# A transformer layer's last chunk: projection, layer norm and MLP in two halves of the queries, with the stores on SyncE's queue

## The reference

```python
h = _layernorm(x, ln1_g, ln1_b)
x = x + _mha(h, h, sa_wq, ...)            # 16 heads of 16, self attention
h = _layernorm(x, ln2_g, ln2_b)
x = x + _mha(h, context, ca_wq, ...)      # cross attention, ends in o @ wo.T + bo
h = _layernorm(x, ln3_g, ln3_b)
h = gelu(h @ mlp_w1.T + mlp_b1) @ mlp_w2.T + mlp_b2   # exact gelu, hidden width 1024
return x + h
```

## Time and profile before

| what | value |
|---|---|
| median of 3 runs | 1604.9 us (1602.36 to 1605.7) |
| time of the profiled execution | 1600.0 us |
| span of the profiled execution | 1598.3 us |
| mean granted TensorE clock over the span | 0.963 of full |
| TensorE busy | 1470.2 us (92%) |
| ScalarE busy | 1068.1 us (67%) |
| VectorE busy | 536.6 us (34%) |

### The profile page before, as it was taken

How to read it: one execution, slowest core, us unless ns; L and a number is a source line. 1 busy time by engine, 2 the same in 40 slices (tenths; PEclk the granted TensorE clock), 3 DMA queues, 4 the chain that set the end, 5 groups by cost and what they waited for, 6 DMA issues and landing times.

```text
span 1598.3 us, 21199 instructions
## 1 busy us (share of the span) xinstructions
PE 1470.2 (92%) x8062; PEld 636.2 (40%) x8062; DVE 536.6 (34%) x1286; ACT 1068.1 (67%) x1285; POOL 44.0 (3%) x62
## 2 busy tenths in 40 slices
PE   8889999998874999999999999699999999999967
PEld 5567777776331222322322322232223432432334
DVE  2445555556541022231330431233232133143140
ACT  2323333332433999999999999589788787797831
POOL 2100000000110000000000000000000000000000
PEclk9999999999896999999999999799899999999988
DMA  7300000000496000010010254501000000000000
GB/s 237 145 7 8 6 7 7 7 3 0 97 249 112 11 21 11 11 39 21 11 37 20 31 84 85 112 21 47 12 21 11 25 11 11 21 15 1 7 7 14
DMA packets 37672, 64.07 MB, mean 40 GB/s; under 512 B 6164, under 2 KB 21844, under 8 KB 37428
## 3 DMA queue, kind: packets, MB, share of 16 engines
q1 hardware_dynamic: 32024, 40.87, 12.3%
q0 software_dynamic: 5552, 21.89, 3.8%
HBM read 40.85 MB, written 22.02 MB: 39 GB/s over the span
## 4 chain that ended last, share of the span: by engine, by line
PE 71%; ACT 17%; DVE 4%; DMA 4%; issue 3%; SPq 0%; DVEq 0%; ACTq 0%; POOL 0%; POOLq 0%
PE PS L954 22%; PE PS L937 15%; ACT PX L677 14%; PE PS L756 6%; PE PS L765 6%; PE PS L1011 5%; PE PS L1023 4%; PE PS L994 2%; PE PS L802 2%; DMA k_parts<-KPARTS 2%; PE PS L728 1%; PE PS L774 1%; PE PS L777 1%; PE PS L973 1%; PE PS L732 1%
## 5 line engine op out<-in xcount | busy, mean ns | idle before, releaser
L677 ACT ACTIVATE PX<-PS 128x1024 f32<-128x1024 f32 (+1 forms) x928 | 883.6, 1040 | 163.5 <-PE PS L937 114.3
L954 PE MATMUL PS<-PX,V 128*32 128x512 f32 (+1 forms) x3712 | 499.4, 610 | 5.0 <-ACT PX L677 3.0
L937 PE MATMUL PS<-QST,stack 50*128 50x512 f32 (+1 forms) x1856 | 385.3, 472 | 44.0 <-DMA stack<-k_parts 22.7
L937 PEld LDWEIGHTS PS<-QST,stack 50*128 50x128 f32 (+1 forms) x1856 | 155.8, 185 | 445.2 <-ACT PX L677 342.6
L954 PEld LDWEIGHTS PS<-PX,V 128*32 128x32 f32 (+1 forms) x3712 | 73.7, 108 | 152.1 <-issue 126.3
L1373 DVE COPY OT<-PS 128x512 f32<-128x512 f32 x32 | 22.1, 692 | 313.0 <-PE PS L954 311.7
L604 ACT ACTIVATE PR<-PS,small 128x1601 f32<-128x1601 f32 x16 | 25.6, 1597 | 106.8 <-DVE small L1210 106.8
L756 PE MATMUL PS<-tokF,XT 128*128 128x512 f32 (+1 forms) x256 | 95.0, 525 | 0.6 <-DVE small L1142 0.6
L765 PE MATMUL PS<-tokT,PT 128*128 128x256 f32 (+1 forms) x416 | 93.3, 381 | 0.6 <-DVE CZ L1259 0.6
L765 PEld LDWEIGHTS PS<-tokT,PT 128*128 128x128 f32 (+1 forms) x416 | 77.9, 190 | 10.7 <-issue 0.8
L1023 PE MATMUL PS<-W,HIDT 128*128 128x256 f32 x256 | 65.2, 404 | 10.6 <-ACT HIDT L663 9.8
(11 more groups left out here) (134 smaller groups left out, 1148.6 us busy)
## 6 DMA issues: line engine op xcount, KB each, us to landing
QST<-q_parts SPq DMA_DIRECT2D x192, 64.0 KB
q_parts<-PARTS POOLq DMA_DIRECT2D x16, 512.0 KB, 5.4
stack<-k_parts SPq DMA_DIRECT2D x24, 256.0 KB, 9.7
stack<-k_parts SPq DMA_DIRECT2D x24, 200.1 KB, 7.1
k_parts<-KPARTS POOLq DMA_DIRECT2D x8, 512.0 KB, 12.2
v_cross<-V POOLq DMA_DIRECT2D x1, 3328.0 KB, 10.0
V<-v_cross SPq DMA_DIRECT2D x2, 1664.0 KB, 13.8
k_parts<-PARTS POOLq DMA_DIRECT2D x6, 512.0 KB, 3.4
```

What stands on the lines that cost most here:

```text
L677: act.activation(PX[0:kr, (2 * t + half) % 4, :, :], PS[0:kr, slot:slot + 2, :], ACT.Exp, scale=SCALE).then_inc(at["exp"], 1)
L937: ins = pe.matmul(PS[0:kr, 2 * (n % LOOK) + jj, :], KST[a][lo:lo + NROW, pair, kt * P:kt * P + kr].bitcast(F32R), QST[lo:lo + NROW, pair, ...
L954: ins = pe.matmul(PS[32 * j:32 * j + 32, 6, :], V[0:kr, kt, 2 * (g // 2 * GH + j) + g % 2, :], PX[0:kr, (2 * t + j // 2) % 4, j % 2, :], s ...
```

## The change

Only the last chunk's tail is rewritten.

- The divide: VectorE takes the reciprocal straight from PSUM and multiplies `ONF`, one half of 256 queries after the other (`END = 256`, `END_TILES = 2`).
- The projection of group 1, bias, residual, statistics, inverse square root and standardisation run per half of two tiles. The square root's twelve small steps are so executed twice.
- The transposes run per half, into banks 4 and 5; the scaling to `HC` moves from VectorE to ScalarE (Identity with scale and bias), 256 columns an instruction.
- W1 is multiplied per half, 16 units of 256 columns in place of 8 of 512, through banks 0, 1, 6 and 7; the second half's transposes stand after six units of the first (`END_EARLY = 6`), and its scaling on ScalarE after six Gelus. There are 16 Gelus of 256 columns.
- The output product writes banks 2 to 5; a tile of the first half waits only for the Gelus of the first half.
- `mlp_b2` is added to the residual `X` beforehand, so one addition per tile is left after the product.
- SyncE issues the last four stores, after all its loads; GpSimd's loop ends a chunk earlier.

The core of the diff:

```diff
+        for i in range(TILES - TPC, TILES):
+            sp.wait_ge(A[1]["out_ready"], i + 1)
+            sp.dma_start(out[i * P:(i + 1) * P, :], XH[:, i % TPC, :]).then_inc(S["end_stored"], 16)
+        sp.wait_ge(S["end_stored"], 16 * TPC)
...
-        with gp.Fori(0, CHUNKS) as c:
+        with gp.Fori(0, CHUNKS - 1) as c:
...
+                def end_scaled(half):
+
+                    for i in range(2):
+                        act.wait_ge(at["hT"], 2 * (q + half) + i + 1)
+                        act.activation(HC[:, i, half * END:(half + 1) * END],
+                                       PS[:, END_TURN + i, half * END:(half + 1) * END], ACT.Identity,
+                                       scale=col("L1_xattn_ln3_g", i), bias=col("L1_xattn_ln3_b", i)) \
+                            .then_inc(at["hc"], 1)
+
+                end_scaled(0)
+                act.wait_ge(at["mlp"], q * TPC)
+                for n in range(2 * units):
+                    half, i = n // units, n % units
+                    if n == END_EARLY:
+                        end_scaled(1)
+                    act.wait_ge(at["unit"], units * q + n + 1)
+                    act.activation(HIDT[:, i, half * END:(half + 1) * END],
+                                   PS[:, END_HIDDEN[n % len(END_HIDDEN)], 0:END], ACT.Gelu,
+                                   bias=col("L1_xattn_mlp_b1", i)).then_inc(at["unit_taken"], 1)
...
+            def end_turn(half):
+
+                pe.wait_ge(at["hat"], q + 1 + half)
+                for i in range(2):
+                    for tt in range(half * END_TILES, (half + 1) * END_TILES):
+                        ins = pe.transpose(PS[:, END_TURN + i, tt * P:(tt + 1) * P],
+                                           XH[:, tt, i * P:(i + 1) * P], ident[:])
+                    ins.then_inc(at["hT"], 1)
+
+            def end_hidden(half, i):
+
+                n = half * units + i
+                if i == 0:
+                    pe.wait_ge(at["hc"], 2 * (q + 1 + half))
+                if n >= len(END_HIDDEN):
+                    pe.wait_ge(at["unit_taken"], units * q + n - len(END_HIDDEN) + 1)
+                for c in range(2):
+                    ins = pe.matmul(PS[:, END_HIDDEN[n % len(END_HIDDEN)], 0:END], W1[:, c, i * P:(i + 1) * P],
+                                    HC[:, c, half * END:(half + 1) * END], start=(c == 0), stop=(c == 1))
+                ins.then_inc(at["unit"], 1)
+
+            pe.wait_ge(at["wop"], 16)
+            pe.wait_ge(at["normed"], CHUNKS * GP - 1)
+            for i in range(TPC):
+                end_projection(0, i)
+            for half in range(2):
+                pe.wait_ge(at["normed"], CHUNKS * GP + half)
+                for i in range(half * END_TILES, (half + 1) * END_TILES):
+                    end_projection(1, i).then_inc(at["y"], 1)
+            end_turn(0)
+            for i in range(units):
+                if i == END_EARLY:
+                    end_turn(1)
+                end_hidden(0, i)
+            for i in range(units):
+                end_hidden(1, i)
+            for tt in range(TPC):
+                pe.wait_ge(at["unit_taken"], units * (q + 1 + tt // END_TILES))
+                for k in range(units):
+                    ins = pe.matmul(PS[:, END_OUT[tt], 0:D], HIDT[:, k, tt * P:(tt + 1) * P], W2[:, k, :],
+                                    start=(k == 0), stop=(k == units - 1))
+                ins.then_inc(at["mlp"], 1)
...
+                for half in range(2):
+                    span = slice(half * END, (half + 1) * END)
+                    ch(ve.reciprocal(REC[:, span], PS[:, 7, span]))
+                    ve.tensor_tensor(ONF[:, 1, span], ONF[:, 1, span], REC[:, span], ALU.mult) \
+                        .then_inc(at["normed"], 1)
+                for half in range(2):
+                    tiles = range(half * END_TILES, (half + 1) * END_TILES)
+                    ve.wait_ge(at["y"], q * TPC + (half + 1) * END_TILES)
...
+                    rsqrt(END_TILES, ch, i=half * END_TILES)
+                    for i in tiles:
+                        ins = ve.tensor_scalar(XH[:, i, :], X[:, q * TPC + i, :], sm(AG + 2 * i), sm(NY + i),
+                                               ALU.subtract, ALU.mult)
+                    ins.then_inc(at["hat"], 1)
...
+                    ins = ve.tensor_tensor(X[:, q * TPC + i, :], X[:, q * TPC + i, :], row("L1_xattn_mlp_b2"), ALU.add)
...
+                    ve.wait_ge(at["mlp"], q * TPC + i + 1)
+                    ve.tensor_tensor(XH[:, i, :], PS[:, END_OUT[i], 0:D], X[:, q * TPC + i, :], ALU.add) \
+                        .then_inc(at["out_ready"], 1)
```

More of the change, by code:

```diff
@@ L74 @@
 LOOK = 3
+END = CHUNK // 2
+END_TILES = TPC // 2
+END_HIDDEN = (0, 1, 6, 7)
+END_TURN = 4
+END_OUT = (2, 3, 4, 5)
+END_EARLY = 6
 class Map:
@@ L235, in build @@
         l0_gates l0_rtanh l0_ubiased l0_utanh l0_rps l0_candps l0_candz l0_cand l0_x1
-        ln1_hat ln1_T ln1_taken qkv_unit v_unit_taken out_stored""".split()
+        ln1_hat ln1_T ln1_taken qkv_unit v_unit_taken out_stored end_stored""".split()
     S = {n: sem(n) for n in names}
@@ L556, in _ @@
                     .then_inc(S["out_stored"], 16)
-        gp.wait_ge(S["out_stored"], 16 * TILES)
+        gp.wait_ge(S["out_stored"], 16 * (TILES - TPC))
     @block.scalar
@@ L685, in _ @@
             if a == 1:
[L687 to L694, removed]
+                q = CHUNKS - 1
+                units = HID // P
+                def end_scaled(half):
[15 more added lines that the diff above has]
+                                   bias=col("L1_xattn_mlp_b1", i)).then_inc(at["unit_taken"], 1)
     @block.tensor
@@ L973, in sums, with piece @@
                 pe.matmul(PS[:, 7, :], spread[:], SUMS[:], start=True, stop=True).then_inc(at["sums"], 1)
-            def piece(kind, i, q, part, tail=False, at=at):
-                whole = part is None
-                first, last = whole or part == 0, whole or part == PARTS_OF[kind] - 1
+            def piece(kind, i, q, part, at=at):
+                first, last = part == 0, part == PARTS_OF[kind] - 1
                 def share(n):
-                    if whole:
-                        return range(n)
                     w = n // PARTS_OF[kind]
                     return range(part * w, (part + 1) * w)
-                bank = i % 4 if tail else 7
                 if kind == "y":
@@ L993, in piece @@
                     for g in share(GP):
-                        ins = pe.matmul(PS[:, bank, 0:D], ONF[:, g, i * P:(i + 1) * P], WOP[:, g, :],
+                        ins = pe.matmul(PS[:, 7, 0:D], ONF[:, g, i * P:(i + 1) * P], WOP[:, g, :],
                                         start=(g == 0), stop=(g == GP - 1))
@@ L1000, in piece @@
                     for tt in range(TPC):
-                        ins = pe.transpose(PS[:, bank, tt * P:(tt + 1) * P],
+                        ins = pe.transpose(PS[:, 7, tt * P:(tt + 1) * P],
                                            XH[:, tt, i * P:(i + 1) * P], ident[:])
@@ L1007, in piece @@
                         pe.wait_ge(at["hc"], 2 * q + 2)
-                        if tail and i >= 4:
-                            pe.wait_ge(at["unit_taken"], HID // P * q + i - 3)
                     for c in share(2):
-                        ins = pe.matmul(PS[:, bank, :], (CAWQ if kind == "u" else W1)[:, c, i * P:(i + 1) * P],
+                        ins = pe.matmul(PS[:, 7, :], (CAWQ if kind == "u" else W1)[:, c, i * P:(i + 1) * P],
                                         HC[:, c, :], start=(c == 0), stop=(c == 1))
@@ L1017, in piece @@
                 if kind == "o":
-                    if tail:
-                        pe.wait_ge(at["unit_taken"], HID // P * CHUNKS)
-                    elif first:
+                    if first:
                         pe.wait_ge(at["gelu"], q + 1)
                     for k in share(HID // P):
-                        ins = pe.matmul(PS[:, bank, 0:D], HIDT[:, k, i * P:(i + 1) * P], W2[:, k, :],
+                        ins = pe.matmul(PS[:, 7, 0:D], HIDT[:, k, i * P:(i + 1) * P], W2[:, k, :],
                                         start=(k == 0), stop=(k == HID // P - 1))
@@ L1069, in _ @@
             sums(CHUNKS, 0)
[L1071 to L1083, removed]
+            q = CHUNKS - 1
+            units = HID // P
+            def end_projection(g, i):
+                return pe.matmul(PS[:, i, 0:D], ONF[:, g, i * P:(i + 1) * P], WOP[:, g, :],
+                                 start=(g == 0), stop=(g == GP - 1))
+            def end_turn(half):
[5 more added lines that the diff above has]
+                    ins.then_inc(at["hT"], 1)
@@ L1415, in standardise, with piece @@
                 ve.wait_ge(at["hat"], q + 1)
-            def piece(kind, i, q, tail=False, a=a, at=at):
+            def piece(kind, i, q, a=a, at=at):
                 if kind in "yo":
@@ L1430, in piece @@
                     ve.wait_ge(at["hT"], 2 * q + i + 1)
```

(33 more changed lines are left out.)

## The result

| | before | after |
|---|---|---|
| median | 1604.84 us (1602.32 to 1607.6, 6 runs) | 1592.55 us (1589.79 to 1594.41, 6 runs) |
| profiled execution, span | 1598.3 us | 1589.8 us |
| instructions | 21199 | 21258 |

The two spans differ by only 8.5 us. The spread sums, up to which both kernels run the same code, begin at 1538.25 in one profiled execution and at 1543.33 in the other. So I measure the tail from the start of the spread sums, and compare whole executions by their medians only.

A forecast was written before the change was run, and what follows sets the result against it. The bound was the last 60 us, a chain stepping from engine to engine with nothing beside it. 6.8 - 0.6 + 0.45 + 0.5 = 7.2 us off 1604.9 gave 1597.7 us, range 1593.8 to 1601.5.

The forecast's parts named there:

- After it: Behind the output product: one addition in place of two, 0.45 us won; last store by SyncE, 0.5 us won.
- Division and projection: From the spread sums to VectorE's layer norm: it starts at about 1543.9 in place of 1546.64, 2.7 us won.
- Layer norm of the first half: On VectorE, for two tiles in place of four: 5.7 us in place of 8.56, 2.85 us won.
- Transposes and scaling: Between the layer norm and W1: 1.8 us in place of 2.94, 1.15 us won.
- W1 and output product: TensorE's stretch from the start of W1: 31.9 us against 31.3 before, 0.6 us lost.
- Cover of the second half: Inside W1: second `hat` is ready 1.4 to 3.7 us before TensorE asks for it, so no wait.
- Table load: On ScalarE: Gelu's load of 1.28 us runs behind the first two scalings, 1551.4 to 1552.7, and costs nothing.
- Identity behind Gelu: Rival, ScalarE's second scalings: Identity outside Gelu's set needs two more loads, 1.28 us each; gain 4.6 to 6.2 us; chance 0.08.
- Weight loads: Rival, W1 in halves: twice-loaded weights no longer hide, 12.2 us more, 1610 us; chance 0.03.
- the slow store: Rival, the end: SyncE's store lands in 4.3 us, gain 5.1 us, 1599.8 us; chance 0.06.
- the clock's: Rival, TensorE's pause before the transposes: clock stays full, gain 10.4 us, 1594.5 us; chance 0.08.
- the first four cases: Chances: forecast holds 0.70, clock stays full 0.08, more table loads 0.08, slower store 0.06.

The follow-up runs named there:

- The run with VectorE: The changed kernel with the scaling into HC given back from ScalarE to VectorE, half by half; 1591.2 us, ratio 0.9917 to the kernel before.

## Why the prediction was wrong, point by point

**The step that failed is "After it", the store's term.** It said "0.5 won", with 0.7 as the most. The closing shrank by 5.7 us in the profiled executions, and the run with the store alone took 0.9968 of the time, 5.1 us less. I had compared two transfers, issue and landing. SyncE's store landed in 1.7 and not 2.2, so that comparison gives 0.94 us (0.74 + 2.0 against 0.1 + 1.7, the 0.1 being my estimate), and it was nearly right as far as it went. What I left out stood in the numbers I had: the store is issued at 1591.22, lands 2.0 later, and the span ends at 1598.3. I had these 5.1 us before me and carried them over as a fixed cost of the program's end. They are GpSimd's: in the kernel after, some 0.4 us lie between the landing of SyncE's last store and the end. The bound of the range came from rows of transfers, and no bound was put on the stretch behind them.

**The other steps held in the main.**

- *Division and projection:* VectorE began the layer norm 5.5 us after the spread sums' start (1548.82, in the timeline) where I had 5.65. The reciprocal from PSUM took 1.77.
- *Layer norm of the first half:* 5.77 measured, 5.7 forecast.
- *Transposes and scaling:* 1.74 measured, 1.8 forecast; two scalings in a row took 1.03. W1 began at 13.04 against 13.15.
- *ScalarE's scaling:* the size was right, but crediting 1.15 us to the step must not be read as the engine's doing. The run with VectorE shows that all of it comes from the halves.
- *W1 and output product:* 30.9 us against 31.9. The second transposes took 0.44 in TensorE's stream and not 1.0, since by then the clock was full and I had sized them by a row at half clock; the output product took 13.83 and not 14.10, W1's forty last records 0.216 each and not 0.22. The 0.35 us lost to narrower matmuls were a slip of my sum: I put 64 records at 0.22 against 32 at 0.43, though twice 0.22 is 0.44. At 0.216, 64 records are 13.8 us, as long as the 13.75 I took for the 32 wide ones. The low clock cost 8.01 - 5.45 = 2.56, forecast 2.7.
- *Cover of the second half:* its `hat` (the signal that `XH` is standardised) was there at 1560.24, TensorE asked at about 1564.2. The cover was 4 us where 1.4 to 3.7 were forecast, and even 1.7 less of it with VectorE's scaling cost nothing.
- *Table load:* mis-placed. It did not start when the scalings ended (1556.3) but 2.2 us later, behind the wait for the first unit, and delayed the first Gelu to 1559.82. It cost nothing, for the reason given: three banks were free. Its price of 1.28 was right.
- *After it, the addition:* one in place of two. From the end of the product to the end of the last addition it is 0.45 us in place of 0.98: 0.53 won, 0.45 forecast.

Up to the last addition the forecast was 6.65 us and 7.8 were measured: 1.0 of the difference is TensorE's stretch.

**The rivals.** The clock fell, as in the forecast, but not as I had reasoned. I had expected it to fall in TensorE's pause, since before it fell 2.9 us into one; after, it stayed full through the whole pause (1550.1 to 1554.63) and fell only at about 1554.75, with the transposes. It rose some 5.2 us after W1 began, where I had taken 4.9. Identity behind Gelu needed no further load: the trace has one table load in the tail. With this the statement of the Trainium skill ("ScalarE: Activation LUTs", Table sets: the hidden batching unit) that the cheap functions are in every set agrees with the trace as far as Identity in Gelu's set goes. Weight loads did not show, at 0.216 us a record. SyncE's store landed in 1.7 us, so the slow store did not happen. None of the rivals had the mechanism that decided, and the only one with a gain above the forecast was the clock's. The chance of 0.89 for "faster" does not follow from its rule either: the first four cases have 0.92 together, and less a tenth that is 0.83.

**What stays open.** What GpSimd does in the 5 us is not in the trace, which has no instruction of it there. That they follow its last instruction or wait, whether or not this is a store, stands in a loop or waits for a landing, is shown; what is done in them is not. Of the parts of the halves only the scaling had a run of its own; what the division, the layer norm, the Gelu and the dropped addition gave is read from the two traces. The 1.3 us between the tails' difference (13.6) and that of the medians (12.3) is within the scatter of the upstream part, and I did not look for its cause.

## What to carry to other kernels

Read what lies between the last instruction of the chain and the end of the span as a term like any other, and ask of each engine when its program ends: here the end came 5 us after GpSimd's last instruction but 0.4 after SyncE's last store had landed, so the engine that closes slowly should be done early and its last duty be given away. In a tail without overlap, halving the tile shortens the wide vector steps but not the fixed ones, and pays as long as TensorE has other work until the second half is there. Measure a tail from an event inside the same execution: the start of this one moved by 5 us between two executions of the same code. Look at the granted clock in it as well, since that alone moved the tail by 1.3 us.

## What the runs showed of the hardware

- GpSimd's end: 4.8 to 5.2 us from its last instruction or wait to the end of the span, in six programs that ended in five different ways (the kernel before and five of the runs). It does not show in the kernel after, where GpSimd's last store starts at 1538.54 and the closing is 2.1 us.
- A pause of TensorE could be filled: 20 records of 256 columns whose results nobody reads (18 of them between projection and transposes, 2 behind the transposes) kept the granted clock at full through a stretch where it was at half before, and the kernel became 2.75 us shorter by its tail.
- Two 256-wide scalings from PSUM with two pointer operands took 1.03 us on ScalarE and 1.01 on VectorE. My half of the 512-wide 0.82, 0.41 each, was too low for VectorE.
- A table load stood behind the wait of the activation that needed it in the kernel after (1558.52), and ahead of it in the kernel before (1535.45). ScalarE's scalings are not the reason: with them taken out, the load still came behind that wait, after 18 us of idleness. What decides between the two stays open.
